# A four-layer transformer on one core: the fourth layer's preparation moved among and behind the third layer's expert blocks, and a tail with two buffers

## The chip, the cores and the metric

The kernel runs on one core of a Trainium2 chip. The metric is device time in microseconds from launch to end; lower is better. Before the change the median of three runs is 1811.25 us (1808.31 to 1811.31).

## The reference, cut to what matters

A token stream `x` of 8 x 256 tokens with 128 features goes through four layers. Each layer adds a cross attention of the normalised tokens and then a feed forward of the normalised result. The change touches the end of the third layer's feed forward (eight experts, two of them for each token) and what the fourth layer needs before its attention can start:

```python
x = x + _L2_ffn_ref(_layernorm(x), gate_w, w1, w3, w2)
#   scores = softmax(x @ gate_w.T); the two best experts, weights p0 and p1
#   each expert: y = (silu(x @ w1.T) * (x @ w3.T)) @ w2.T
#   result per token: p0 * y_first + p1 * y_second
x = x + _L3_xattn_ref(_layernorm(x), ctx_768, mask, g_norm, null_kv, Wq, Wkv, Wout, g_out)
x = x + _L3_ffn_ref(_layernorm(x), W_fc, b_fc, A_fc, B_fc, W_proj, b_proj, A_proj, B_proj)
#   W_fc and W_proj: rounded to 8 bits with one scale each, plus a low rank term
```

## The kernel before, in words

Each engine has a program of its own, and semaphores order them. TensorE (`pe`), ScalarE (`act`), VectorE (`dve`), GpSimd (`pool`) and SyncE (`sp`) run through the same list: `attention(n)`, `feed_forward(n)`, then `early(n + 1)` (the parts of the next layer that don't need its tokens), then on TensorE and ScalarE `ffn_end(n)` (the last normalised tokens), then `boundary`, where all wait for all. An engine executes its instructions in the order in which they are written; a wait holds everything behind it on that engine.

**The blocks.** The third layer's feed forward (`routed_by_token`, L1336 for GpSimd, L1551 ScalarE, L2051 TensorE, L2703 VectorE) works on 39 blocks of 128 token rows, each belonging to one expert. For a block, SyncE loads the rows (`block_rows_at`, L994, L1004), TensorE turns them (L1647, a transposition), ScalarE rounds them to f16 (L1409), VectorE takes the remainder (L2731), TensorE multiplies with two weight matrices (18 matmuls), ScalarE takes the silu (L1568), VectorE the product (L2736), TensorE multiplies with the third matrix (3 matmuls, which the profile records as 6), VectorE copies the result to SBUF (`y_of`, L2758), and GpSimd stores it to its tokens' places in HBM with an indirect DMA (L1342). Rings of eight hold the rows and the results: SyncE loads block i into a place only when the store of block i - 8 has landed, since the store takes its addresses from that place, and VectorE copies result i only when store i - 8 has landed.

**The token tail.** When all stores have landed, SyncE loads the results back, 512 tokens (a chunk) at a time, two transfers each (L1011), with two places in SBUF. For each of the four chunks VectorE forms the sum in `xnew` (L2747, L2751, four instructions each), takes the statistics (L2262, L2267, into `mv`) and copies `xnew` to `x` (L2756); GpSimd turns the variance into a factor (L1072, L1073) and writes the normalised rows to `yn` (L1076, four instructions); TensorE turns them into bank 6 (`turn_rows`, L1922); ScalarE writes them to `xnT` (`ffn_ln_evac`, L879). `xnew`, `mv` and `yn` exist once: VectorE waits for `yn` of a chunk before the next chunk's sum.

**The fourth layer's preparation.** `early(ATT[3])` comes behind the tail on VectorE and GpSimd. On TensorE it starts when three of the four chunks are in `xnT` (a wait in `attention`, L1735, on `f.lne`), because the tail's turns stand ahead of it; `ffn_end` then turns the fourth chunk behind it. In it:
- VectorE takes the largest absolute value of a weight part for each partition (L2368), and GpSimd takes it across partitions (`partition_all_reduce`, L1113); VectorE forms scales from it (`value_scale`, `values_scale_and_ones`, L2376), for which ScalarE and VectorE wait to evacuate the values.
- TensorE fills two key and two value tiles; ScalarE and VectorE evacuate them.
- `prep3_operands` (L2334) on VectorE: two maxima (L2336, L2337), for which GpSimd's second `partition_all_reduce` (L1116) waits, two copies, a product and a sum for the null key (L2343, L2345), two small ones, and the rounding of two weights in three instructions each (L2351 to L2353).
- `prep_fill` (L1675) and `evacuate_prep` (L2392): five fills on TensorE in the order bfc, bpr, nv, fc, pr, each evacuated by ScalarE (bfc, nv, pr) or VectorE (bpr, fc). fc and pr take 8 matmuls each, in the profile 16 records, half of them with 16 rows, and wait for the rounded weights.

Of the kernel before, what the change touches and what calls it, by code (L numbers as in the profile page):

```python
# [311 lines left out]
def build(nc, a, out):  # L312
    ctx = ExitStack()
    with ctx:
# [177 lines left out]
        yg2 = Qf[:, 1568:3616].rearrange("p (c j t d) -> p c j t d", j=2, t=4, d=D)  # L492
        yb2 = PTs[:, :, :].rearrange("p u s -> p (u s)")[:, 0:1024].rearrange("p (r d) -> p r d", d=D)
# [531 lines left out]
        def _(pool):  # L1025
# [82 lines left out]
            def early(A):  # L1108
                if A.n == 0:
                    first_context(A)  # L1110
                if A.n == 3:
                    pool.wait_ge(vmax3_rows, 1)
                    pool.partition_all_reduce(vmaxall[:, 3:4], vmax[:, 3:4], P, RMAX).then_inc(vmax3_max, 1)  # L1113

                    pool.wait_ge(prep3_rows, 1)
                    pool.partition_all_reduce(amx, am, P, RMAX).then_inc(prep3_max, 1)  # L1116
# [219 lines left out]
            def routed_by_token(F):  # L1336
# [3 lines left out]
                for i in range(nb):  # L1340
                    need(pool, r.y_read, i + 1)
# [3 lines left out]
                for c in range(NCH):  # L1345
                    if c:
                        need(pool, s.lnf, c)
                    normalise(4, s.stats, c + 1, s.yn, 1.0 + EPS, EPS * EPS, link)
# [54 lines left out]
        def _(act):  # L1403
# [147 lines left out]
            def routed_by_token(F):  # L1551
# [18 lines left out]
                for c in range(NCH - 1):  # L1570
                    need(act, s.lnf, c + 1)
                    ffn_ln_evac(F, move, c).then_inc(s.lne.sem, 1)
# [50 lines left out]
            def ffn_end(F):  # L1623

                s = ffn_s[F.n]
                need(act, s.lnf, NCH if F.n == 2 else NCH + 1)
                ffn_ln_evac(F, move, NCH - 1).then_inc(s.lne.sem, 1)
# [13 lines left out]
        def _(pe):  # L1641
# [93 lines left out]
            def attention(A, early=None):  # L1735
# [9 lines left out]
                elif A.n:  # L1745

                    f = ffn_s[A.n - 1]
                    need(pe, f.lne, NCH - 1 if A.n == 3 else NCH)
# [173 lines left out]
            def turn_rows(F, c):  # L1922
# [128 lines left out]
            def routed_by_token(F):  # L2051
# [188 lines left out]
        def _(dve):  # L2240
# [93 lines left out]
            def prep3_operands():  # L2334
                dve.wait_ge(prep3_zero, 1)
                dve.tensor_reduce(am[:, 0:1], fcn, AX.X, ALU.max, apply_absolute_value=True)  # L2336
                dve.tensor_reduce(am[:, 1:2], prn, AX.X, ALU.max,  # L2337
                                  apply_absolute_value=True).then_inc(prep3_rows, 1)
                dve.tensor_copy(NVflat[0:64, 0:128:18], nv_col[0:64, 0:1].to_broadcast([64, 8]))
                dve.tensor_copy(NVflat[64:128, 1:128:18],  # L2340
                                nv_col[64:128, 0:1].to_broadcast([64, 8])).then_inc(prep3_done, 1)
                q3 = qtmp.rearrange("p (h e) -> p h e", e=64)
                link(dve.tensor_tensor(q3, L3Wq.rearrange("p (h e) -> p h e", e=64),  # L2343
                                       nk_bc[:, :].unsqueeze(1).to_broadcast([P, 16, 64]), ALU.mult))
                link(dve.tensor_reduce(Wn, q3, AX.X, ALU.add))  # L2345
                dve.wait_ge(prep3_max, 1)
                link(dve.tensor_scalar(qsc, amx, 1.0 / 127.0, None, ALU.mult))
# [566 lines left out]
```

## Time and profile before

| | us |
|---|---|
| median of 3 runs | 1811.25 |
| the profiled execution's own time | 1810.04 |
| its span, first to last instruction | 1808.2 |
| last expert matmul ends | 1304.6 |
| first chunk's sum starts | 1311.5 |
| the last chunk is in `xnT` | 1377.05 |
| fourth layer's queries start | 1377.14 |

Engine names: PE is TensorE's matmuls, PEld its weight loads, DVE VectorE, ACT ScalarE, POOL GpSimd, SPq SyncE's DMA queue. Times are from the span's start. A timeline row gives start, duration, engine, line, operation, output and inputs, the count of merged instructions, and in brackets the engine's idle time before it and what ended it.

### The profile page before, as it was taken

How to read it: one execution, taken by the hardware profiler on the slowest of the kernel's cores; microseconds unless marked ns; L12 is line 12 of the kernel's file. 1: busy time of each engine (PE TensorE's matmuls, PEld its weight loads, DVE VectorE, ACT ScalarE, POOL GpSimd, SP SyncE). 2: the span in 40 equal slices, each digit the busy share in tenths (PEclk: the TensorE clock that was granted, in tenths of full speed). 3: DMA queues.
4: the chain of work that ended last, by engine and by line, in shares of the span. 5: the costliest groups of instructions: out<-in, count | busy, mean ns of one | idle time of the engine just before them, and what ended most of it. 6: DMA issues, size and time to landing. Idle time of an engine off the chain costs nothing. (4 is left out here: it accounts for less than half of the span.)

```text
span 1808.2 us, 38603 instructions
## 1 busy us (share of the span) xinstructions
PE 1438.6 (80%) x12662; PEld 1092.6 (60%) x12662; DVE 1105.0 (61%) x2873; ACT 835.5 (46%) x1870; POOL 417.5 (23%) x743
## 2 busy tenths in 40 slices
PE   4989999978999679999628347378728988888977
PEld 2667777756666468887416235356515766667765
DVE  4757777775666668888421136623244888887761
ACT  1545665554333357777315223122203666656542
POOL 2000000011000323332030245723230122222221
PEclk9999999999999889999759768589957999999989
DMA  8980000000000300000011002111110000000000
GB/s 231 284 25 0 0 0 0 0 1 1 1 0 0 96 1 1 0 0 1 1 35 45 24 12 61 40 44 46 45 34 1 2 1 0 0 0 0 1 1 24
DMA packets 81168, 47.91 MB, mean 26 GB/s; under 512 B 27497, under 2 KB 74226, under 8 KB 80882
## 3 DMA queue, kind: packets, MB, share of 16 engines
q1 hardware_dynamic: 77778, 39.86, 10.2%
q0 software_dynamic: 3296, 6.82, 1.1%
q8 instruction: 56, 0.92, 0.2%
q14 instruction: 38, 0.31, 0.1%
HBM read 26.52 MB, written 20.14 MB: 26 GB/s over the span
## 5 line engine op out<-in xcount | busy, mean ns | idle before, releaser
L1451 ACT ACTIVATE Pm<-bank,negm 128x256 f32<-128x256 f32 x784 | 322.5, 473 | 309.6 <-DVE negm L2454 219.6
L1643 PE MATMUL bank<-kT,Qz 64*128 64x256 f32 (+2 forms) x1568 | 298.2, 404 | 10.9 <-ACT Pm L1451 7.4
L2465 DVE TENSOR_TENSOR PTs<-bank,PTs 128x512 f16<-128x512 f32 x384 | 251.4, 683 | 33.3 <-ACT PTs L1409 32.2
L1647 PE MATMUL bank<-ident,Pm 128*128 128x128 f32 x1568 | 230.8, 283 | 43.8 <-DVE PTs L2465 39.2
L1647 PEld LDWEIGHTS bank<-ident,Pm 128*128 128x128 f32 x1568 | 175.8, 143 | 114.4 <-issue 80.1
L1643 PEld LDWEIGHTS bank<-kT,Qz 64*128 64x128 f32 (+1 forms) x1568 | 183.5, 189 | 84.4 <-issue 49.7
L2454 DVE TENSOR_REDUCE negm<-bank 128x2 f32<-128x512 f32 x264 | 176.5, 687 | 79.8 <-PE bank L1643 77.2
L1409 ACT ACTIVATE PTs<-bank 128x512 f16<-128x512 f32 (+1 forms) x388 | 218.7, 604 | 3.5 <-PE bank L1647 3.4
L1643 PEld LDWEIGHTS bank<-VxF,PTs 128*128 128x128 f16 (+1 forms) x4672 | 183.4, 100 | 11.4 <-DVE PTs L2465 3.4
L1643 PE MATMUL bank<-VxF,PTs 128*128 128x65 f16 (+3 forms) x4672 | 187.9, 189 | 2.5 <-DVE PTs L2465 2.4
L1643 PE MATMUL bank<-Qz,R 128*128 128x128 f16 x978 | 92.5, 231 | 29.0 <-ACT Qz L1409 25.1
L1643 PEld LDWEIGHTS bank<-Qz,R 128*128 x978 | 70.1, 99 | 57.5 <-issue 44.9
L1643 PE MATMUL bank<-xHL,R 128*128 (+1 forms) x432 | 99.2, 379 | 0.9 <-DVE Qz L2846 0.8
L1647 PE MATMUL bank<-ident,yn 128*128 128x128 f32 x120 | 27.9, 347 | 90.2 <-POOL yn L1076 86.2
L2451 DVE TENSOR_REDUCE negm<-bank 128x2 f32<-128x512 f32 x128 | 88.2, 689 | 17.4 <-PE bank L1643 15.5
L1129 POOL TENSOR_TENSOR Qz<-xnT,headmask 128x1024 f32<-128x1024 f32 x32 | 60.5, 1894 | 147.3 <-PE bank L1643 129.3
L1643 PE MATMUL bank<-xnT,R 128*128 (+2 forms) x288 | 88.0, 435 | 8.2 <-DVE VxF L795 6.2
L1076 POOL TENSOR_SCALAR yn<-xnew,mv,rstd 128x128 f32<-128x128 f32 x112 | 90.2, 813 | 9.4 <-POOL rstd L1073 9.4
L1643 PEld LDWEIGHTS bank<-R,Qz 128*128 128x128 f32 x704 | 84.1, 192 | 11.1 <-ACT Qz L1611 6.4
L1072 POOL TENSOR_SCALAR ve<-mv 128x2 f32<-128x2 f32 (+1 forms) x44 | 8.9, 203 | 354.3 <-DVE mv L2267 327.7
L1643 PE MATMUL bank<-R,Qz 128*128 128x128 f32 x704 | 85.1, 276 | 3.1 <-ACT Qz L1611 3.1
L1604 ACT ACTIVATE Pm<-bank,upback 128x512 f32<-128x512 f32 x72 | 49.6, 689 | 78.0 <-PE bank L1643 77.8
(327 smaller groups left out, 2168.1 us busy)
## 6 DMA issues: line engine op xcount, KB each, us to landing
token_rows_by_expert<-trash SPq DMA_DIRECT2D x5, 1782.0 KB, 17.9
Qz<-token_rows_by_expert SPq DMA_DIRECT2D x39, 66.0 KB
token_rows_by_expert<-wpad SPq DMA_DIRECT2D x10, 256.0 KB, 4.2
R<-in_L_ffn_ew SPq DMA_DIRECT2D x2, 1024.0 KB, 7.2
R<-in_L_ffn_w SPq DMA_DIRECT2D x1, 2048.0 KB, 9.6
Qz<-expert_rows_by_token SPq DMA_DIRECT2D x8, 256.0 KB, 3.3
R<-in_L_xattn_Wkv SPq DMA_DIRECT2D x2, 768.0 KB, 6.6
Qz<-token_rows_by_expert SPq DMA_DIRECT2D x23, 64.0 KB
```

The source lines that it names most:

```text
L1072: chain(pool.tensor_scalar(ve[:, 0:n], mv[:, at:at + n, 1], scale, offset, ALU.mult, ALU.add))
L1076: last = pool.tensor_scalar(yn[:, at + t, :], xnew[:, at + t, :], mv[:, at + t, 0:1], rstd[:, t:t + 1], ALU.subtract, ALU.mult)
L1129: pool.tensor_tensor(Qz[:, h:h + 4, :], xnT[:, bass.ts(bw, S)].unsqueeze(1).to_broadcast([P, 4, S]), headmask[:, h:h + 4].unsqueeze(2).to_ ...
L1409: return act.activation(dst, src, ACT.Copy, scale=1.0 if gain is None else gain)
L1451: last = act.activation(Pm[:, k % 4, qt * S:(qt + 1) * S], bank[k % 2][:, qt * S:(qt + 1) * S], ACT.Exp, bias=negm[:, k % 4, qt:qt + 1])
L1604: act.activation(sg[0:M, u % 2, :], bank[u % 2][0:M, :], ACT.Silu, scale=upback[0:M, F.n:F.n + 1]).then_inc(s.silu.sem, 1)
L1643: return pe.matmul(o, l, r, start=start, stop=stop)
L1647: return pe.transpose(o, i, ident[0:n, 0:n])
L2451: chain(dve.tensor_reduce(nm, v, AX.X, ALU.max, negate=True))
L2454: dve.tensor_reduce(nm, v, AX.X, ALU.max, negate=True).then_inc(s.negmax.sem, 1)
L2465: dve.tensor_tensor(PTl[:, k % 4, :], bank[2 + k % 2][:, :], PTh[:, k % 4, :], ALU.subtract).then_inc(s.pt[1].sem, 1)
```

## The change

VectorE's `early` parts for the fourth layer become `prep3_part(i)`, called once at the end of each block's iteration on VectorE; most numbers of i do nothing. GpSimd's two `partition_all_reduce` stand ahead of its store of block 10. TensorE's and ScalarE's handling of all four chunks of the tail moves behind `early(ATT[3])`, VectorE's `token_tail` too; GpSimd's part stays where it was. In numbers: `prep3_part` 3 is L2368, 4 and 5 the maxima L2336 and L2337, 6 the two small copies, 7 and 8 L2343 and L2345, 20 and 21 the scales, 22 to 27 the rounding (the old `prep3_operands` is cut up for it and left out below). Sums, statistics and normalised rows have two buffers, so that VectorE and GpSimd each wait for the chunk before the last one.

```diff
@@ -490,6 +490,10 @@
+        mv8 = sb("mv8", [P, 2, 4, 2])
+        spare = PTs[:, :, :].rearrange("p u s -> p (u s)")
+        xn8 = (xnew, spare[:, 1024:1536].rearrange("p (t d) -> p t d", d=D))
+        yn8 = (yn, spare[:, 1536:2048].rearrange("p (t d) -> p t d", d=D))
@@ -1108,12 +1112,6 @@
             def early(A):
                 if A.n == 0:
                     first_context(A)
-                if A.n == 3:
-                    pool.wait_ge(vmax3_rows, 1)
-                    pool.partition_all_reduce(vmaxall[:, 3:4], vmax[:, 3:4], P, RMAX).then_inc(vmax3_max, 1)
-
-                    pool.wait_ge(prep3_rows, 1)
-                    pool.partition_all_reduce(amx, am, P, RMAX).then_inc(prep3_max, 1)
@@ -1338,14 +1336,26 @@
                 for i in range(nb):
+                    if i == 10:
+                        pool.wait_ge(vmax3_rows, 1)
+                        pool.partition_all_reduce(vmaxall[:, 3:4], vmax[:, 3:4], P, RMAX).then_inc(vmax3_max, 1)
+                        pool.wait_ge(prep3_rows, 1)
+                        pool.partition_all_reduce(amx, am, P, RMAX).then_inc(prep3_max, 1)
                     need(pool, r.y_read, i + 1)
                     pool.indirect_dma_start(out=ytok, out_offset=bass.IndirectOffsetOnAxis(
                         ap=xb2[:, i % RING, D:D + 1].bitcast(U32), axis=0),
...
                 for c in range(NCH):
-                    if c:
-                        need(pool, s.lnf, c)
-                    normalise(4, s.stats, c + 1, s.yn, 1.0 + EPS, EPS * EPS, link)
+                    need(pool, s.stats, c + 1)
+                    plain(pool)
+                    link(pool.tensor_scalar(ve[:, 0:4], mv8[:, c % 2, :, 1], 1.0 + EPS, EPS * EPS, ALU.mult, ALU.add))
+                    link(pool.tensor_tensor(rstd[:, 0:4], ve[:, 0:4], neghalf[:, 0:4], ALU.pow))
+                    need(pool, s.lnf, c - 1)
+                    plain(pool)
+                    for t in range(4):
+                        last = pool.tensor_scalar(yn8[c % 2][:, t, :], xn8[c % 2][:, t, :], mv8[:, c % 2, t, 0:1],
+                                                  rstd[:, t:t + 1], ALU.subtract, ALU.mult)
+                    last.then_inc(s.yn.sem, 1)
@@ -1567,9 +1577,6 @@
-                for c in range(NCH - 1):
-                    need(act, s.lnf, c + 1)
-                    ffn_ln_evac(F, move, c).then_inc(s.lne.sem, 1)
@@ -1623,6 +1630,10 @@
                 s = ffn_s[F.n]
+                if F.n == 2:
+                    for c in range(NCH - 1):
+                        need(act, s.lnf, c + 1)
+                        ffn_ln_evac(F, move, c).then_inc(s.lne.sem, 1)
                 need(act, s.lnf, NCH if F.n == 2 else NCH + 1)
                 ffn_ln_evac(F, move, NCH - 1).then_inc(s.lne.sem, 1)
@@ -1745,7 +1756,7 @@
-                    need(pe, f.lne, NCH - 1 if A.n == 3 else NCH)
+                    need(pe, f.lne, 0 if A.n == 3 else NCH)
                     if A.n - 1 in ROUTED:
@@ -1924,7 +1935,7 @@
-                    last = turn(bank[6][:, t * P:(t + 1) * P], yn[:, t, :])
+                    last = turn(bank[6][:, t * P:(t + 1) * P], (yn8[c % 2] if F.n == 2 else yn)[:, t, :])
                 last.then_inc(s.lnf.sem, 1)
@@ -1933,6 +1944,11 @@
+                if F.n == 2:
+                    for c in range(NCH - 1):
+                        need(pe, ffn_s[F.n].lne, c)
+                        turn_rows(F, c)
+                    need(pe, ffn_s[F.n].lne, NCH - 1)
                 turn_rows(F, NCH - 1)
@@ -2099,14 +2115,6 @@
-                for c in range(NCH - 1):
-                    if c:
-                        need(pe, s.lne, c)
-                    else:
-                        need(pe, r.high, nb)
-                        need(pe, r.low, nb)
-                    turn_rows(F, c)
@@ -2331,26 +2339,42 @@
-            def prep3_operands():
...
+            def prep3_part(i):
+                if i == 3:
+                    loaded(dve, "l3")
+                    dve.wait_ge(prep3_zero, 1)
+                    dve.tensor_reduce(vmax[0:DC, 3:4], L3Wkv[:, 1024:2048], AX.X, ALU.max,
+                                      apply_absolute_value=True).then_inc(vmax3_rows, 1)
+                elif i == 4:
+                    dve.tensor_reduce(am[:, 0:1], fcn, AX.X, ALU.max, apply_absolute_value=True)
+                elif i == 5:
+                    dve.tensor_reduce(am[:, 1:2], prn, AX.X, ALU.max,
+                                      apply_absolute_value=True).then_inc(prep3_rows, 1)
+                elif i == 6:
...
+                elif i == 7:
+                    link(dve.tensor_tensor(q3, L3Wq.rearrange("p (h e) -> p h e", e=64),
...
+                elif i == 8:
+                    link(dve.tensor_reduce(Wn, q3, AX.X, ALU.add))
+                elif i == 20:
+                    dve.wait_ge(prep3_max, 1)
+                    link(dve.tensor_scalar(qsc, amx, 1.0 / 127.0, None, ALU.mult))
+                    link(dve.reciprocal(rqs, qsc))
+                elif i == 21:
+                    values_scale_and_ones(ATT[3])
+                elif 22 <= i < 28:
+                    n, w = (i - 22) // 3, (fcn, prn)[(i - 22) // 3]
+                    if (i - 22) % 3 == 0:
+                        link(dve.tensor_scalar(w, w, rqs[:, n:n + 1], ROUND, ALU.mult, ALU.add))
+                    elif (i - 22) % 3 == 1:
+                        link(dve.tensor_scalar(w, w, -ROUND, 127.0, ALU.add, ALU.min))
+                    else:
...
@@ -2363,13 +2387,7 @@
             def early(A):
-                if A.n == 3:
-                    loaded(dve, "l3")
-                    dve.tensor_reduce(vmax[0:DC, 3:4], L3Wkv[:, 1024:2048], AX.X, ALU.max,
-                                      apply_absolute_value=True).then_inc(vmax3_rows, 1)
                 attention(A, ("early",))
-                if A.n == 3:
-                    prep3_operands()
                 if A.n in prep:
                     evacuate_prep(A)
@@ -2423,7 +2441,7 @@
-                        if kinds == "early" and (kind, k) == ("v", 0):
+                        if kinds == "early" and (kind, k) == ("v", 0) and A.n != 3:
                             values_scale_and_ones(A)
@@ -2738,22 +2756,33 @@
                     if i >= 2:
                         y_of(r, i - 2)
+                    prep3_part(i)
                 y_of(r, nb - 1)
+            def token_tail(F):
...
                 for c in range(NCH):
-                    need(dve, s.yn, c)
+                    xn = xn8[c % 2]
+                    need(dve, s.yn, c - 1)
                     dve.wait_ge(r.tail[c % 2], 16 * 2 * (c // 2 + 1))
                     for t in range(4):
-                        last = dve.scalar_tensor_tensor(xnew[:, t, :], yg2[:, c % 2, 0, t, :], c_p0[:, 4 * c + t:4 * c + t + 1],
+                        last = dve.scalar_tensor_tensor(xn[:, t, :], yg2[:, c % 2, 0, t, :], c_p0[:, 4 * c + t:4 * c + t + 1],
...
                         last.then_inc(r.added.sem, 1)
                     need(dve, r.added, 4 * c + 4)
-                    stats(xnew, 4, link, s.stats.sem)
-                    link(dve.tensor_copy(x[:, 4 * c:4 * c + 4, :], xnew[:, :, :]))
+                    plain(dve)
+                    for t in range(4):
+                        last = dve.bn_stats(st6[:, t, :], xn[:, t, :])
+                    link(last)
+                    for t in range(4):
+                        last = dve.bn_aggr(mv8[:, c % 2, t, :], st6[:, t, :])
+                    last.then_inc(s.stats.sem, 1)
+                    dve.tensor_copy(x[:, 4 * c:4 * c + 4, :], xn[:, :, :])
@@ -2893,6 +2922,8 @@
                     early(ATT[n + 1])
+                    if n == 2:
+                        token_tail(FFN[n])
                     boundary(dve, "dve", n + 2)
```

## Rows read from the trace of the kernel before

**Rows 1.** The timeline, last block: its last expert matmuls.
```profile
1303.68 0.93 PE L1643 MATMUL bank<-R,Pm 128*128 x6 [0.48 <-DVE Pm L2736]
```
**Rows 2.** The timeline, token tail: chunk one, starts of chunks two and four.
```profile
1307.66 15.82 SPq L1011 DMA_DIRECT2D Qz<-expert_rows_by_token  x8
1311.52 1.14 DVE L2747 SCALAR_TENSOR_TENSOR xnew<-Qz,OT,x 128x128 f32<-128x128 f32 x4 [6.58 <-DMA Qz<-expert_rows_by_token]
...
1315.47 0.19 POOL L1072 TENSOR_SCALAR ve<-mv 128x4 f32<-128x4 f32 x1 [9.24 <-DVE mv L2267]
...
1317.01 3.13 POOL L1076 TENSOR_SCALAR yn<-xnew,mv,rstd 128x128 f32<-128x128 f32 x4 [0.22 <-POOL rstd L1073]
1320.23 1.14 DVE L2747 SCALAR_TENSOR_TENSOR xnew<-Qz,OT,x 128x128 f32<-128x128 f32 x4 [4.66 <-issue]
...
1337.93 1.14 DVE L2747 SCALAR_TENSOR_TENSOR xnew<-Qz,OT,x 128x128 f32<-128x128 f32 x4 [4.62 <-issue]
```
**Rows 3.** The timeline, preparation of the fourth layer: fills, first reduce, evacuation of fc.
```profile
1339.90 3.75 PE L1643 MATMUL bank<-ctxT,R 97*128 97x256 f32 x8 [0.83 <-issue]
...
1343.89 3.78 PE L1643 MATMUL bank<-R,ctxb 96*128 96x512 f32 x4 [0.24 <-DVE kT L2252]
...
1352.23 0.38 POOL L1113 PARTITION_ALL_REDUCE vmaxall<-vmax  x1 [5.71 <-issue]
...
1356.34 1.23 PE L1647 MATMUL bank<-ident,R 128*16 128x128 f32 x5 [8.66 <-DVE VxF L795]
...
1358.02 3.51 PE L1643 MATMUL bank<-R 128*16 128x128 f32 x16 [0.46 <-ACT R L1409]
...
1368.77 0.69 DVE L2252 COPY R<-bank 128x512 f32<-128x512 f32 x1 [5.15 <-PE bank L1643]
```
**Rows 4.** The timeline, last chunk's turn and evacuation, first queries.
```profile
1375.21 1.12 PE L1647 MATMUL bank<-ident,yn 128*128 128x128 f32 x4 [0.69 <-ACT R L1409]
1376.36 0.69 ACT L1410 ACTIVATE xnT<-bank,vecT 128x512 f32<-128x512 f32 x1 [1.21 <-PE bank L1647]
1377.14 5.14 PE L1643 MATMUL bank<-xnT,R 128*128 128x256 f32 x12 [0.81 <-ACTq L665]
```
**Rows 5.** The timeline at full clock: a key fill, a value fill.
```profile
1384.23 1.13 PE L1643 MATMUL bank<-ctxT,R 97*128 97x256 f32 x4
...
1389.78 1.02 PE L1643 MATMUL bank<-R,ctxb 96*128 96x512 f32 x2
```
**Rows 6.** Windows: length, busy of PE PEld DVE ACT POOL, PEclk, DMA share, GB/s.
```profile
1304.60:1306.60 2.00, 0.01 (x1) 0.00 (x0) 0.29 (x1) 0.00 (x0) 1.33 (x2) 1.00 0.10 33
1365.00:1374.50 9.50, 9.50 (x27) 6.49 (x26) 0.69 (x1) 0.00 (x0) 0.00 (x0) 0.50 0.00 0
1374.50:1381.50 7.00, 5.50 (x15) 4.25 (x15) 0.00 (x0) 2.43 (x4) 0.40 (x1) 0.50 0.01 2
```
**Rows 7.** The timeline, the third layer's attention: VectorE and GpSimd at the same time.
```profile
1109.79 0.45 DVE L2502 TENSOR_TENSOR xnew<-rtmp,x 128x256 f32<-128x256 f32 x1
1109.79 1.82 POOL L1076 TENSOR_SCALAR yn<-xnew,mv,rstd 128x128 f32<-128x128 f32 x2 [0.22 <-POOL rstd L1073]
```
**Rows 8.** Within the blocks, timeline: product, turn, store, load; tile view: all stores.
```profile
1212.91 0.62 DVE L2736 SCALAR_TENSOR_TENSOR Pm<-bank,upback,Pm 128x384 f32<-128x384 f32 x1 [2.11 <-ACT Pm L1568]
...
1213.04 0.27 PE L1647 MATMUL bank<-ident,Qz 128*128 128x128 f32 x1
...
1214.00 0.96 POOL L1342 DMA_INDIRECT expert_rows_by_token<-PTs,Qz  x1 [2.22 <-DVE PTs L2762]
...
1216.47 0.34 SPq L1004 DMA_DIRECT2D Qz<-token_rows_by_expert  x1
...
L1342 POOL DMA_INDIRECT expert_rows_by_token<-PTs,Qz x39: 959/960/988, 1189.4 to 1305.3; - x39
```
**Rows 9.** VectorE's longest part in the timeline, and a window over most parts.
```profile
1357.66 1.23 DVE L2343 TENSOR_TENSOR R<-R,nk_bc 128x1024 f32<-128x1024 f32 x1
...
1356.11:1363.44 7.33, 4.74 (x21) 2.75 (x21) 7.01 (x16) 0.85 (x2) 0.39 (x1) 0.64 0.00 0
```

More of the change, by code:

```diff
@@ L2332, in _ @@
             boundary(dve, "dve", 1)
-            def prep3_operands():
[L2335 to L2341, printed above, removed]
-                q3 = qtmp.rearrange("p (h e) -> p h e", e=64)
[L2343 to L2347, printed above, removed]
-                link(dve.reciprocal(rqs, qsc))
-                for i, w in enumerate((fcn, prn)):
-                    link(dve.tensor_scalar(w, w, rqs[:, i:i + 1], ROUND, ALU.mult, ALU.add))
-                    link(dve.tensor_scalar(w, w, -ROUND, 127.0, ALU.add, ALU.min))
-                    dve.tensor_scalar(w, w, -128.0, qsc[:, i:i + 1], ALU.max, ALU.mult).then_inc(prep3_done, 1)
@@ new lines, in prep3_part @@
+            def prep3_part(i):
+                q3 = qtmp.rearrange("p (h e) -> p h e", e=64)
+                if i == 3:
[9 more added lines that the diff above has]
+                elif i == 6:
+                    dve.tensor_copy(NVflat[0:64, 0:128:18], nv_col[0:64, 0:1].to_broadcast([64, 8]))
+                    dve.tensor_copy(NVflat[64:128, 1:128:18],
+                                    nv_col[64:128, 0:1].to_broadcast([64, 8])).then_inc(prep3_done, 1)
+                elif i == 7:
+                    link(dve.tensor_tensor(q3, L3Wq.rearrange("p (h e) -> p h e", e=64),
+                                           nk_bc[:, :].unsqueeze(1).to_broadcast([P, 16, 64]), ALU.mult))
+                elif i == 8:
[13 more added lines that the diff above has]
+                    else:
+                        dve.tensor_scalar(w, w, -128.0, qsc[:, n:n + 1], ALU.max, ALU.mult).then_inc(prep3_done, 1)
@@ L2740, in routed_by_token @@
                         y_of(r, i - 2)
+                    prep3_part(i)
                 y_of(r, nb - 1)
+            def token_tail(F):
+                s, r = ffn_s[F.n], routed_s[F.n]
                 for c in range(NCH):
-                    need(dve, s.yn, c)
+                    xn = xn8[c % 2]
+                    need(dve, s.yn, c - 1)
                     dve.wait_ge(r.tail[c % 2], 16 * 2 * (c // 2 + 1))
                     for t in range(4):
-                        last = dve.scalar_tensor_tensor(xnew[:, t, :], yg2[:, c % 2, 0, t, :], c_p0[:, 4 * c + t:4 * c + t + 1],
+                        last = dve.scalar_tensor_tensor(xn[:, t, :], yg2[:, c % 2, 0, t, :], c_p0[:, 4 * c + t:4 * c + t + 1],
                                                         x[:, 4 * c + t, :], ALU.mult, ALU.add)
@@ L2750, in routed_by_token @@
                     for t in range(4):
-                        last = dve.scalar_tensor_tensor(xnew[:, t, :], yg2[:, c % 2, 1, t, :], c_p1[:, 4 * c + t:4 * c + t + 1],
-                                                        xnew[:, t, :], ALU.mult, ALU.add)
+                        last = dve.scalar_tensor_tensor(xn[:, t, :], yg2[:, c % 2, 1, t, :], c_p1[:, 4 * c + t:4 * c + t + 1],
+                                                        xn[:, t, :], ALU.mult, ALU.add)
                         last.then_inc(r.added.sem, 1)
                     need(dve, r.added, 4 * c + 4)
-                    stats(xnew, 4, link, s.stats.sem)
-                    link(dve.tensor_copy(x[:, 4 * c:4 * c + 4, :], xnew[:, :, :]))
+                    plain(dve)
[6 more added lines that the diff above has]
+                    dve.tensor_copy(x[:, 4 * c:4 * c + 4, :], xn[:, :, :])
             def y_of(r, j):
```

## Prediction

> **What bounds the kernel now.** I read the page first: no engine is full, so a stage has to be read by its own waits. Then the timeline from the last expert matmul to the first query. The last expert matmuls end at 1304.6 [rows 1], and the fourth layer's queries start at 1377.14 [rows 4]: 72.5 us, and nothing of the fourth layer's attention can start before their end. Two chains stand one behind the other in it. The first is the token tail [rows 2]: the stored rows come back at 1311.5, and from one chunk's sum to the next are (1337.93 - 1311.52) / 3 = 8.8 us, in which VectorE works 3.95 us (1311.52 to 1315.47), GpSimd 4.67 us (1315.47 to 1320.14), and each waits for the other, since `xnew` and `yn` exist once. The second is the preparation [rows 3]: it begins at 1339.9 on TensorE, and until 1375.2 [rows 4] it is a chain through all engines, with 5.71 us before the `partition_all_reduce` in which GpSimd shows no instruction. TensorE's clock is at 0.50 in nearly all of it [rows 6], that is at 1.2 GHz of 2.4. The blocks before it are another matter: there TensorE sets a period of (1305.3 - 1189.4) / 38 = 3.05 us, and VectorE waits 2.11 us at a stretch in each [rows 8].
>
> **The change, part by part.** The sum is made from 1304.6, the end of the blocks, to the queries' start, and compared with 72.5 us.
>
> VectorE's parts among the blocks. A part stands behind the copy of a result and ahead of the remainder L2731 of the next block. That remainder is next used by the following period's matmuls, nearly a period later, and the product L2736 comes after an idle stretch of 2.11 us [rows 8]. The longest part takes 1.23 us [rows 9], so each fits; I cost them at nothing. Without that cover they would cost 7.33 us for the window over most parts [rows 9], 1.2 for L2368 (as large as L2343), 1.15 for the scales, together 9.7 us.
>
> GpSimd's hold at block 10. The two reductions stand ahead of store 10. Their price is 5.71 + 0.38 [rows 3], then about 0.8 for the second and gaps: 7 us, if the second doesn't pay 5.7 again. Store 9 would end near 1218, store 10 start near 1225 instead of 1220. What waits: SyncE's load of block 18 and VectorE's copy 18. Store 8 starts at 1214.0 and the load of block 16 at 1216.5 [rows 8]; VectorE is then two blocks behind TensorE's turns, so the turn of block 11 is the one at 1213.04, and that of block 16 comes five periods later, at 1228.3. A load lands within 3 us, so the slack is about 9 us; a hold that delays store 10 by 5 us is hidden. With a second 5.7 us it would be 10.7, a loss of 1 to 2 us. Nothing taken; the removed 5.71 + 0.38 at the old place are in the 72.5.
>
> The preparation, now directly behind the blocks. TensorE's fills start at about 1304.8. Unmoved at the old speed they are: keys 3.75, values 3.8, evacuation of the last value 1.8 (two instructions of 0.9 on ScalarE, then VectorE), bfc and bpr to nv's start 1.7 (1356.34 to 1358.02), nv 3.5, fc 16 records at 9.50 / 27 = 0.35 us, so 5.6, and VectorE's evacuation 0.7 [rows 3, 6]: 20.9 us, so that VectorE is free at 1325.7. At full clock a key fill is 1.13 and a value fill 1.02 [rows 5], so 2.3 and 2.0, nv half, fc 3.4 (half and a start): 13.8 us, free at 1318.6. Which clock? It stays at 1.00 for two us after the last matmul [rows 6], and now TensorE goes on working; but in the same preparation fc and pr ran at 0.50 although TensorE was busy all 9.50 us [rows 6]. So I take the fills at full clock and fc at half, the row nearest to it, free at 1320.7. pr follows on TensorE and is hidden by the tail. The rows from HBM (1311.5) are there before that: their latency costs nothing now.
>
> The tail with two buffers. VectorE's 4.2 us for a chunk (with the copy) is now beside GpSimd's 4.67, and GpSimd's is longer. With 0.1 for a wait: 3.95 + 4 x 4.75 = 22.95, then 0.15, the turn 1.12, the evacuation 0.69 and 0.1 to the queries [rows 4]: 25.0 us. The loads of chunks three and four wait for `added` of the chunk two before (2.3 us into it) and take 4 us: hidden.
>
> VectorE and GpSimd now work at once, as they never did in the tail. In the third layer's attention they do [rows 7]: two L1076 beside a VectorE instruction with two inputs in SBUF took 1.82 us, where two in the tail take 1.57 [rows 2], so 0.25 us more for 0.45 us of VectorE. VectorE's sums are 2.3 us a chunk, with the copy 2.7. If GpSimd lost all of it for three chunks it would be 8 us, at the least nothing. By that ratio [rows 7] it would be up to 1.5 a chunk, but only part of the sums falls beside L1076; I take 0.7 a chunk, 2.1 us.
>
> The clock after it. TensorE is now idle in most of the tail. Before, it rose only at 1381.5, 4.4 us after the queries' start, although fc and pr had gone before [rows 6]. It can come later now. Between 0 and 3 us (the queries' 5.14 us [rows 4] at half clock, and some more), I take 1.
>
> The sum: 1304.6 + 16.1 (preparation) + 25.0 + 2.1 = 1347.8, against 1377.1: 29.3 us less, less 1 for the clock: 28.3. Against the profiled execution's own time, 1810.04, that gives 1781.7; the median, 1811.25, is 1.2 above it, and gives 1783. I predict 1782.5. Own bounds: full clock, no contention, no loss, 33.5 less, 1777; half clock throughout, contention and 3 us of clock, 1304.8 + 20.9 + 25.0 + 8 = 1358.7, so 15.4 less, 1796; not all of these fall together, so about 1776 to 1790.
>
> **The rivals.**
>
> *The tail doesn't overlap.* VectorE's two input sums and GpSimd's normalisation exclude each other, so that a chunk still costs near 8.8 us. For it: the longer L1076 [rows 7]. Against it: there only a part of VectorE's time was lost. The tail is then 3 x 8.8 + 8.6 + 2.1 = 37.1 instead of 27.1: 10 us less gained, 1792.5. The Trainium skill (SBUF — State Buffer, "Who interferes with whom") says that a VectorE instruction with two SBUF inputs contends with a GpSimd instruction that reads SBUF, through a shared read interface held for the whole instruction. By that rule as a strict lock, all of the sums and the copy would come on top of GpSimd's time, 8 us for three chunks where I take 2.1, and the sum would be 1788.5; the trace shows a part of it [rows 7].
>
> *The blocks grow.* The parts aren't free among the blocks, 9.7 us, or the hold is longer than its cover. For it: the store's engine holds for 7 us, and VectorE's parts stand ahead of L2731, which TensorE waits for. Against it: idle 2.11 us in each period. 1782.5 + 9.7 = 1792.
>
> *Slower than before: the clock stays down.* TensorE idles from about 1326 to 1348 but for turns, and the fourth layer's first batch, which begins behind it, runs at 1.2 GHz. To eat 28 us, matmuls that are busy 28 us at full clock would have to take double: a stretch at half clock of some 60 us behind the queries' start instead of 4.4. In the rows the longest such stretch is 1365.0 to 1381.5, 16.5 us [rows 6]. At 70 us it would give about 1815.
>
> *The change doesn't do what it says.* A wait left ahead of the preparation would keep it behind the tail. `need` with the value 0 gives no wait, the loads of the fourth layer's weights stand ahead of the blocks' loads in SyncE's program, and the memsets that part 3 waits for stand ahead of the stores in GpSimd's. Only the two buffers would be left, three times 8.8 - 4.75, 12 us less: 1799. Very small.
>
> **How the numbers follow.** The forecast 0.68; the tail without overlap 0.14; the blocks grow 0.10; the preparation kept behind 0.02; the clock 0.03; unnamed small mixtures of the first three 0.03. The range must take in the first rival's neighbourhood in part: 1774 to 1792 leaves out the far ends of both rivals and what is above, about 0.2. A measurement of this kernel can tell about 0.2%, 3.6 us, from no change; only the clock case ends above that, and of what I can't name 0.01 within it: faster 0.96, same 0.01, slower 0.03.
>
> **What would show it.** In the changed profile: the block period still 3.05 us and the last expert matmul near 1304.6; a gap in GpSimd's stores behind store 9 of about 8 us with the next four close together, and no later turn waiting for a load; the key fills directly behind the last block with the clock at 1.00; the first sum near 1321 with nothing waited for but fc's evacuation; sums and normalisation side by side with a period near 5.5 us, set by GpSimd; queries near 1348. It would be wrong if the first sum stands behind 1326, if L1076's successor takes well over 0.8 us each, if the period is near 8, or if the clock rises more than 8 us behind the queries' start.

## The result, and where the time went

The changed kernel takes 1789.88 us (median of 4 runs, 1787.96 to 1791.18), the kernel before 1811.2 beside it: ratio 0.988, 95% interval 0.9867 to 0.9893. The time lies within the range, but of the 28.7 us that the prediction took off, 21.3 came. So the question is where 7.4 us went.

I read the timeline over the same stretch as before, from the last expert matmul to the first query. TensorE's part of the preparation, now directly behind the blocks:

```profile
1307.48 0.93 PE L1654 MATMUL bank<-R,Pm 128*128 x6 [0.48 <-DVE Pm L2754]
1308.25 1.89 PE L1654 MATMUL bank<-ctxT,R 97*128 97x256 f32 x8
...
1315.14 3.56 PE L1654 MATMUL bank<-R 128*16 128x128 f32 x16 [0.56 <-ACT R L1419]
...
1321.55 0.48 PE L1654 MATMUL bank<-R 16*128 16x128 f32 x2
...
1321.96 0.80 PE L1654 MATMUL bank<-ident,R 128*128 128x128 f32 x2
1322.07 0.69 DVE L2260 COPY R<-bank 128x512 f32<-128x512 f32 x1 [7.17 <-PE bank L1654]
1322.68 1.13 DVE L2770 SCALAR_TENSOR_TENSOR xnew<-Qz,OT,x 128x128 f32<-128x128 f32 x4
```

The last expert matmuls end at 1308.41. The key fills stand right behind them and take 1.89 us instead of 3.75 [rows 3]: full clock. The windows (the number behind the five engines is the granted clock) show that it isn't kept throughout:

```profile
1308.40:1315.10 6.70, 4.35 (x18) 2.24 (x16) 2.89 (x7) 2.76 (x6) 1.32 (x2) 1.00 0.41 117
1315.10:1318.50 3.40, 3.36 (x16) 2.24 (x16) 0.00 (x0) 0.00 (x0) 0.00 (x0) 0.50 0.42 117
1318.50:1322.00 3.50, 3.50 (x19) 2.40 (x17) 0.00 (x0) 0.27 (x1) 0.00 (x0) 0.99 0.00 0
```

nv runs at half clock and takes 3.56 us, as before (3.51 [rows 3]). fc falls into the stretch at full clock behind it, where a pair of matmuls takes 0.48 to 0.49 us; from 1321.96 on, in pr, a pair takes 0.80 again. The first sum stands directly behind VectorE's evacuation of fc (a line with no wait in brackets), 14.3 us behind the last expert matmul. Then the tail, GpSimd and the two ends of the chain:

```profile
1326.04 0.38 DVE L2783 BATCH_NORM_AGGREGATE mv<-st 128x2 f32<-128x6 f32 x4
...
1333.67 0.19 POOL L1351 TENSOR_SCALAR ve<-mv 128x4 f32<-128x4 f32 x1 [23.65 <-issue]
...
1335.22 3.16 POOL L1356 TENSOR_SCALAR yn<-xnew,mv,rstd 128x128 f32<-128x128 f32 x4 [0.22 <-POOL rstd L1352]
1338.41 1.14 DVE L2770 SCALAR_TENSOR_TENSOR xnew<-Qz,OT,x 128x128 f32<-128x128 f32 x4 [7.72 <-POOL yn L1356]
...
1343.53 1.14 DVE L2770 SCALAR_TENSOR_TENSOR PTs<-Qz,OT,x 128x128 f32<-128x128 f32 x4 [0.95 <-POOL PTs L1356]
...
1345.28 3.74 POOL L1356 TENSOR_SCALAR yn<-xnew,mv,rstd 128x128 f32<-128x128 f32 x4 [0.24 <-POOL rstd L1352]
...
1350.65 3.12 POOL L1356 TENSOR_SCALAR PTs<-PTs,mv,rstd 128x128 f32<-128x128 f32 x4 [0.24 <-POOL rstd L1352]
...
1355.04 0.69 ACT L1420 ACTIVATE xnT<-bank,vecT 128x512 f32<-128x512 f32 x1 [4.06 <-PE bank L1658]
1359.86 4.33 PE L1654 MATMUL bank<-xnT,R 128*128 128x256 f32 x12 [4.86 <-POOLq L669]
```

Here are both losses. First, the statistics of chunk one are there at 1326.42, but the first factor L1351 starts at 1333.67, and "issue" says that nothing in the profile is waited for: 7.0 us beyond a usual 0.2. Second, the last xnT ends at 1355.73, but the queries start at 1359.86 and wait for POOLq L669; before, they waited for ACTq L665, 0.09 us behind it [rows 4]. The view by line of these two lines names them:

```profile
L1351 POOLq MODIFY_POOL_CONFIG  x2: 11/11/11, 1326.7 to 1326.7; - x2
...
L669 POOLq DRAIN  x1: 8934/8934/8934, 1350.7 to 1350.7; - x1
```

I take the idle time behind MODIFY_POOL_CONFIG for the loading of the code of another group of GpSimd operations; experiments 1, 3 and 5 test it. The record alone isn't the price: at 163.05 one stands 0.13 us ahead of the tensor_scalar at 163.18. The reductions among the blocks had loaded their code; the stores behind them need none, and the first tensor_scalar after them loads its own back. It starts to do so at 1326.65, because the wait for the statistics stands ahead of it in GpSimd's program. The kernel before shows the same way back in its second layer, with a reduction at 916.05 and nothing but indirect DMAs between it and this row:

```profile
1034.71 0.19 POOL L1072 TENSOR_SCALAR ve<-mv 128x4 f32<-128x4 f32 x1 [7.13 <-issue]
```

Without a reduction ahead of them the 39 stores cost nothing of the kind: the first factor of the kernel before waits for its statistics alone [rows 2].

At the layer's boundary, the second loss, every engine waits for the drains of all; GpSimd's ends near 1359.7, 5.9 us behind its last instruction (1353.77). Before, a drain of 6.3 us stood there too, from 1357.4, beside the chain of the preparation, where nobody waited for it.

GpSimd among the blocks, the hold at block 10:

```profile
1220.90 0.96 POOL L1345 DMA_INDIRECT expert_rows_by_token<-PTs,Qz  x1 [2.13 <-DVE PTs L2791]
1228.32 0.38 POOL L1341 PARTITION_ALL_REDUCE vmaxall<-vmax  x1 [6.46 <-issue]
1228.61 0.44 POOL L1343 PARTITION_ALL_REDUCE R<-R  x1
1229.24 1.20 POOL L1345 DMA_INDIRECT expert_rows_by_token<-PTs,Qz  x1 [0.19 <-issue]
...
1233.38 0.96 POOL L1345 DMA_INDIRECT expert_rows_by_token<-PTs,Qz  x1 [0.41 <-DVE PTs L2791]
```

From store 9 to store 10 are 8.3 us; with store 13 it has caught up, and no turn waited. The period is (1309.06 - 1193.36) / 38 = 3.04 us, as before, with the clock at 1.00 in all of it: VectorE's parts are hidden.

In one sum, over the two profiled executions: from the last expert matmul's end to the queries 72.5 us became 51.45, 21.1 less; from there to the end of the span 431.1 became 429.6, 1.4 less; ahead of the last expert matmul the new execution is 3.8 us later, and 3.7 of it are there already at the first load of a block. The stages ahead of that load were not changed, and over all kernels here but experiment 5 the end of the last expert matmul scatters between 1302.8 and 1308.4 us. So I compare stretches from the last expert matmul on, beside the times.

### The profile page after: what moved, and what is told of

It is laid out like the page before. It is cut to its first block, busy times and chain, and to the rows that moved or that the text cites. A ratio compares the mean times of both kernels' runs of the same rounds, so it can differ in the third digit from the quotient of the medians.

```text
span 1789.5 us, 38608 instructions
## 1 busy us (share of the span) xinstructions
PE 1435.3 (80%) x12662; PEld 1092.5 (61%) x12662; DVE 1104.2 (62%) x2873; ACT 833.5 (47%) x1870; POOL 418.3 (23%) x743
## 3 DMA queue, kind: packets, MB, share of 16 engines
q1 hardware_dynamic: 77778, 39.86, 10.2%
## 4 chain that ended last, share of the span: by engine, by line
PE 58%; DVE 16%; issue 11%; POOL 6%; ACT 5%; SPq 1%; POOLq 1%; DMA 1%; DVEq 0%; ACTq 0%
PE bank L1654 48%; PE bank L1658 10%; DVE PTs L2483 3%; DVE negm L2469 2%; DVE negm L2472 2%; DVE VxF L799 1%; ACT Pm L1461 1%; SPq L893 1%; POOL token_rows_by_expert L1141 1%; DVE st L2270 1%; ACT PTs L1419 1%; ACT Pm L1552 1%; POOL token_rows_by_expert L1312 1%; ACT Qz L1419 1%; POOL yn L1080 1%
## 5 line engine op out<-in xcount | busy, mean ns | idle before, releaser
L1654 PEld LDWEIGHTS bank<-R,Qz 128*128 128x128 f32 x704 | 84.1, 192 | 11.1 <-ACT Qz L1618 6.4
L1419 ACT ACTIVATE Qz<-bank 128x128 f16<-128x128 f32 (+1 forms) x102 | 41.7, 409 | 95.9 <-PE bank L1658 72.9
```

The lines of the kernel that those rows point to most:

```text
L1419: return act.activation(dst, src, ACT.Copy, scale=1.0 if gain is None else gain)
L1654: return pe.matmul(o, l, r, start=start, stop=stop)
```

## The experiments

All start from the changed kernel. "Stretch" is the time from the last expert matmul's end to the queries' start, in the profiled execution: 51.45 us in the changed kernel. Beside experiments 1 to 4 the kernel before took 1809.03 us (median of 7), beside experiments 5 to 8 1810.41 (of 9); each ratio is to the kernel before beside it.

**1. Load the code back early.** One small tensor_scalar on GpSimd behind the last store; its result is overwritten before it is read.

```diff
                         in_=yb2[:, i % RING, :], in_offset=None).then_inc(r.stored[i % RING].sem, 16)
+                link(pool.tensor_scalar(ve[:, 0:4], neghalf[:, 0:4], 1.0, 0.0, ALU.mult, ALU.add))
                 for c in range(NCH):
```

> The changed kernel with one small tensor_scalar added on GpSimd behind its last store, where it then idles for over 20 us. Theory (code swap): in the changed kernel the first factor of the tail starts 7.0 us after the statistics it waits for, and a MODIFY_POOL_CONFIG stands in that gap, because the two reductions among the blocks left other code on GpSimd. The small instruction takes this gap into the idle stretch: the first factor follows its statistics within 0.3 us, the tail is 7 us shorter, about 1783 us. Rival (the indirect DMAs are still being finished, or GpSimd is slow to wake after a long wait): the gap stays, the same 1790 us.

GpSimd in its timeline:

```profile
1311.70 0.19 POOL L1348 TENSOR_SCALAR ve<-neghalf 128x4 f32<-128x4 f32 x1 [6.93 <-issue]
1320.95 0.20 POOL L1352 TENSOR_SCALAR ve<-mv 128x4 f32<-128x4 f32 x1 [9.05 <-DVE mv L2784]
```

The 6.93 us of "issue" now stand beside TensorE's fills, and the first factor starts 0.2 us behind its statistics. Stretch 45.2 us, 6.2 less. Time 1782.68 us (1780.9 to 1789.07, 4 runs), ratio 0.9863 (0.9837 to 0.989). The queries still wait 4.86 us for POOLq L669.

**2. Drain early.**

```diff
                         in_=yb2[:, i % RING, :], in_offset=None).then_inc(r.stored[i % RING].sem, 16)
+                pool.drain()
                 for c in range(NCH):
```

> The changed kernel with one more drain on GpSimd behind its last store, ahead of the tail. Theory (drain pays for indirect DMAs): GpSimd's drain at the boundary ends 5.9 us after its last instruction, with 71 indirect DMAs since the drain before; at the third layer's boundary 2.7 us with 32; at the second none with none: about 0.083 us each. With a drain in the idle stretch the one at the boundary ends with the last instruction, and the queries start 4.1 us earlier, right behind the last evacuation: about 1786 us. Rival (a drain on GpSimd costs about 6 us there by itself): nothing changes at the boundary, 1790 us.

The boundary's drain and the queries:

```profile
L669 POOLq DRAIN  x1: 3121/3121/3121, 1349.7 to 1349.7; - x1
```

```profile
1332.63 0.19 POOL L1352 TENSOR_SCALAR ve<-mv 128x4 f32<-128x4 f32 x1 [23.54 <-issue]
...
1354.75 2.50 PE L1655 MATMUL bank<-xnT,R 128*128 128x256 f32 x5 [0.81 <-ACTq L669]
```

The boundary's drain is now as long as the last yn beside it, and the queries wait for ScalarE again. The load of the code is still there. Stretch 47.3 us, 4.2 less. Time 1785.93 us (1780.52 to 1788.59, 4 runs), ratio 0.986 (0.9834 to 0.9886); by the times alone it could not be told from experiment 1.

**3. Both**, the drain first, then the small instruction.

> Both additions together, drain and then the small tensor_scalar. If both theories hold the gains add: 7.0 + 4.1 = 11.1 us, about 1779 us, and from the last expert matmul to the queries there are 40.3 us instead of 51.4. By the rivals between 1783 and 1790.

```profile
1317.24 0.19 POOL L1349 TENSOR_SCALAR ve<-neghalf 128x4 f32<-128x4 f32 x1 [12.78 <-issue]
1320.65 0.20 POOL L1353 TENSOR_SCALAR ve<-mv 128x4 f32<-128x4 f32 x1 [3.21 <-DVE mv L2785]
...
1322.21 3.91 POOL L1358 TENSOR_SCALAR yn<-xnew,mv,rstd 128x128 f32<-128x128 f32 x4 [0.22 <-POOL rstd L1354]
...
1327.89 3.77 POOL L1358 TENSOR_SCALAR PTs<-PTs,mv,rstd 128x128 f32<-128x128 f32 x4 [0.21 <-POOL rstd L1354]
...
1333.45 3.74 POOL L1358 TENSOR_SCALAR yn<-xnew,mv,rstd 128x128 f32<-128x128 f32 x4 [0.24 <-POOL rstd L1354]
...
1338.83 3.13 POOL L1358 TENSOR_SCALAR PTs<-PTs,mv,rstd 128x128 f32<-128x128 f32 x4 [0.24 <-POOL rstd L1354]
```

12.78 us of "issue", the drain's 5.9 and the code's 6.9, lie in GpSimd's idle time, and 3.21 us of it are left ahead of the first factor. Stretch 41.2 us: 10.3 less, where the two alone gave 6.2 + 4.2 = 10.4. They add up, so each was a cost of its own. Time 1779.98 us (1776.97 to 1782.3, 4 runs), ratio 0.9841 (0.9822 to 0.986).

**4. How long is the drain for what?** The drain ahead of store 0 instead, so that of the layer's 71 indirect DMAs the 32 that spread the token rows over the experts are drained early and the 39 stores are not.

```diff
                 for i in range(nb):
+                    if i == 0:
+                        pool.drain()
```

> The changed kernel with one more drain on GpSimd ahead of its store of block 0, none behind the stores. 39 indirect DMAs then lie between it and the boundary's drain. Theory (0.083 us each): the boundary's drain ends 3.2 us after the last normalised row instead of 5.9, and the queries start 2.6 us earlier against the last evacuation. Rival (a drain before takes the whole cost away, or none of it): 0 or 5.9 us.

```profile
L669 POOLq DRAIN  x1: 6313/6313/6313, 1346.7 to 1346.7; - x1
```

It ends at 1353.0, the last yn at 1349.8: 3.3 us behind it. With the 71 of the changed kernel it is 5.9, with the 32 at the third layer's boundary 2.7, with the 32 ahead of the new drain here 2.7 again, with none 0.1. So about 0.083 us for each indirect DMA issued since the drain before. All of them move 128 rows, so these runs can't tell a count of DMAs from a count of rows. Stretch 49.0 us, 2.4 less, where 2.6 was expected. One run, 1786.51 us.

**5. A longer hold.** Experiment 3, and the small tensor_scalar between the two reductions, so that the code is changed three times at block 10.

```diff
                         pool.partition_all_reduce(vmaxall[:, 3:4], vmax[:, 3:4], P, RMAX).then_inc(vmax3_max, 1)
+                        link(pool.tensor_scalar(ve[:, 0:4], neghalf[:, 0:4], 1.0, 0.0, ALU.mult, ALU.add))
                         pool.wait_ge(prep3_rows, 1)
```

> The kernel with both additions, and one more small tensor_scalar between the two reductions at block 10, so that GpSimd swaps its code three times there: about 20 us of hold instead of 8. It tests the slack that I gave the loads. Theory (a load may come 9 us late): store 10 is 18 us late instead of 5, and the blocks lose 18 - 9 = 9 us, in one gap before the turn of block 18. Rival (the ring of eight covers it, or the store is on the chain at once): no loss, or 13 us more than now.

```profile
1225.43 0.38 POOL L1341 PARTITION_ALL_REDUCE vmaxall<-vmax  x1 [5.98 <-issue]
...
1233.57 0.19 POOL L1343 TENSOR_SCALAR ve<-neghalf 128x4 f32<-128x4 f32 x1 [7.77 <-issue]
...
1239.55 0.37 POOL L1344 PARTITION_ALL_REDUCE R<-R  x1 [5.79 <-issue]
1240.12 1.20 POOL L1346 DMA_INDIRECT expert_rows_by_token<-PTs,Qz  x1 [0.19 <-issue]
...
1244.63 0.45 PE L1661 MATMUL bank<-ident,Qz 128*128 128x128 f32 x1 [8.37 <-DMA Qz<-token_rows_by_expert]
1245.53 2.10 PE L1657 MATMUL bank<-Qz,R 128*128 128x128 f16 x18 [0.45 <-ACT Qz L1422]
```

Each change of code costs 5.8 to 7.8 us, in either direction, and no indirect DMA stands between them. Store 10 starts at 1240.1 instead of near 1221.6 without any hold (store 9 at 1218.5 and one period), so 18.5 us late, and the turn of block 18 waits 8.37 us for its load, where 9 was worked out. From the first store to the last are 124.2 us instead of 115.8 in experiment 3. So the chain store, load, turn is as the prediction took it, and the slack is about 10 us where it had 9. Behind the gap the 18 matmuls take 2.10 us instead of 1.6: the granted clock is 0.50 from 1241.0 to 1251.2. One run, 1784.68 us against 1779.98 for experiment 3: the blocks' 8.4 us don't show in full, since in that execution the stretch is 1.6 us shorter (39.6) and the part behind it 2.4 (428.8 instead of 431.2).

**6. Take the first chunk ahead.** Experiment 3 has GpSimd idle until the first statistics, which wait for fc's evacuation. Here VectorE takes the first chunk between the evacuations of bpr and of fc, and the small instruction stands ahead of store 20, where the stores have slack.

```diff
+                    if i == 20:
+                        link(pool.tensor_scalar(ve[:, 0:4], neghalf[:, 0:4], 1.0, 0.0, ALU.mult, ALU.add))
...
-                if A.n in prep:
+                if A.n == 3:
+                    evacuate_prep(A, 2)
+                    token_tail(FFN[2], (0,))
+                    evacuate_prep(A, 5, 2)
+                elif A.n in prep:
                     evacuate_prep(A)
```

> The kernel with both additions, and two more edits: VectorE does the first chunk's sum and statistics between its evacuations of bpr and fc, where it idles for 7 us, and GpSimd's small tensor_scalar stands ahead of store 20, so that the code swap lies among the blocks. Theory (the tail is a chain of GpSimd's four normalisations, 20 us, behind the first statistics): the first sum starts when its rows have come back, about 6.9 us behind the last expert matmul instead of 13.9, and the whole tail is 7 us earlier: 33 us from the last expert matmul to the queries, about 1773 us. Rival (the preparation on TensorE, or the turns behind it, sets the end): the first turn waits for the fills, and no more than 2 us are won, 1778 us or more.

```profile
1309.82 1.12 DVE L2777 SCALAR_TENSOR_TENSOR xnew<-Qz,OT,x 128x128 f32<-128x128 f32 x4
...
1313.74 0.19 POOL L1354 TENSOR_SCALAR ve<-mv 128x4 f32<-128x4 f32 x1 [9.25 <-DVE mv L2790]
...
1316.12 0.69 DVE L2263 COPY R<-bank 128x512 f32<-128x512 f32 x1 [2.27 <-PE bank L1657]
1316.73 1.17 DVE L2777 SCALAR_TENSOR_TENSOR PTs<-Qz,OT,x 128x128 f32<-128x128 f32 x4
...
1320.82 0.19 POOL L1354 TENSOR_SCALAR ve<-mv 128x4 f32<-128x4 f32 x1 [2.20 <-DVE mv L2790]
```

Stretch 35.7 us, 5.5 less than experiment 3 where 8 was expected: the second chunk's sum now waits for fc (1316.12), so GpSimd idles 2.2 us behind the first. Of the expectation's two cases, the tail's chain set most of the gain and the preparation the rest. No turn waits behind the small instruction at store 20. Time 1772.49 us (1770.83 to 1774.18, 5 runs), ratio 0.979 (0.9776 to 0.9804): faster than both kernels, and the best of this study.

**7. No overlap.** Experiment 3 with the sum of a chunk behind the normalisation of the one before, the buffers still two.

```diff
-                    need(dve, s.yn, c - 1)
+                    need(dve, s.yn, c)
```

> The kernel with both additions, but VectorE waits for the normalised rows of the chunk before, as with single buffers. It prices the two buffers. Theory (two buffers hide VectorE's 4 us under GpSimd's 5): the period goes from 5.4 back to 8.7 us, three times 3.3, 10 us slower than with both additions, about 1790 us, and L1358's four instructions take 3.13 us each time instead of 3.7 to 3.9, since nothing runs beside them. Rival (VectorE and GpSimd exclude each other): 3 us slower or less.

```profile
1325.75 3.16 POOL L1358 TENSOR_SCALAR yn<-xnew,mv,rstd 128x128 f32<-128x128 f32 x4 [0.22 <-POOL rstd L1354]
1328.95 1.14 DVE L2772 SCALAR_TENSOR_TENSOR PTs<-Qz,OT,x 128x128 f32<-128x128 f32 x4 [4.62 <-POOL yn L1358]
...
1337.56 1.14 DVE L2772 SCALAR_TENSOR_TENSOR xnew<-Qz,OT,x 128x128 f32<-128x128 f32 x4 [4.56 <-POOL PTs L1358]
```

The period is 8.6 us (8.8 in the kernel before), VectorE waits 4.6 us for GpSimd and GpSimd 4.0 for VectorE, and the stretch is 50.8 us, 9.6 more than in experiment 3. Time 1786.27 us (1784.2 to 1787.9, 4 runs), ratio 0.986 (0.9842 to 0.9878): 6.3 us more than experiment 3 by the medians, 3.4 by the ratios, whose intervals overlap, so the 9.6 rest on the profiles. It is also the measure of the contention: alone, a chunk's four instructions take 3.12 to 3.16 us.

**8. VectorE's parts without spreading.** Experiment 3 with parts 3 to 8 all at block 8.

```diff
-                    prep3_part(i)
+                    if i == 8:
+                        for part_ in range(3, 9):
+                            prep3_part(part_)
+                    elif i > 8:
+                        prep3_part(i)
```

> The kernel with both additions, but VectorE's six parts 3 to 8 all at block 8, 5.5 us at once instead of 1.3 at most. Theory (cover of one period: the remainder is needed 2.8 us after it ends, and VectorE's idle stretch is 2.1 us): TensorE waits once, by 5.5 - 2.8 = 2.7 us, and the blocks grow by that. Rival (the parts are paid whatever their place): no change, since they were paid before; or all 5.5 us show.

```profile
1212.00 1.22 DVE L2365 TENSOR_REDUCE R<-R 128x16 f32<-128x1024 f32 x1
1213.25 0.29 DVE L2751 TENSOR_TENSOR Qz<-bank,Qz 128x128 f16<-128x128 f32 x1
...
1213.74 2.10 PE L1656 MATMUL bank<-Qz,R 128*128 128x128 f16 x18 [2.96 <-DVE Qz L2751]
```

TensorE waits 2.96 us for the remainder that stands behind the parts, and the granted clock is 0.50 from 1212.9 to 1219.7, about two blocks. From store to store are 6.1, 3.3 and 3.3 us (starts 1208.41, 1214.54, 1217.84, 1221.11) instead of 3 x 3.1, about 3.4 us lost; from the first store to the last it is 118.6 us instead of 115.8 in experiment 3, 2.8 more, where 2.7 was expected. The one run's time, 1779.95 us, doesn't show it: the start of the stage scatters by as much. It is the cover that makes the parts free: one at a time fits in VectorE's idle stretch, six don't.

## Why the prediction was right, and what it missed

**The mechanism held.** The parts among the blocks cost nothing (period unchanged, and experiment 8 shows the price without spreading). The hold at block 10 was hidden (8.3 us from store to store, forecast about 8), with the slack near what was worked out (experiment 5: about 10 us, 9 worked out). The preparation came directly behind the blocks, and the tail overlaps (experiment 7: 9.6 us are its worth, where the first rival put 10).

**The step that failed: GpSimd's change of code was costed once.** The prediction priced the 5.7 us ahead of the reductions at block 10 and asked what the stores behind them wait for, but not what GpSimd must do to get from the reductions back to tensor_scalar. In the kernel before, the reductions stood behind the last yn, and that way back lay outside the path. There a copy ran without it (1377.21, 0.4 us), the load began at 1377.64 and the next tensor_tensor, at 1386.08, waited for VectorE anyway. Moved ahead of the tail, it falls into the first chunk: 7.0 us. Experiment 1 takes it away and gets 6.2 back. The price could have been read ahead of the change, from the second layer's 7.13 us. The Trainium skill (GPSIMD Engine Reference, "2.1 Instruction dispatch") says that the first call of freshly loaded code pays a load of some 6 us without a visible instruction; the traces agree, with 5.7 to 7.8 us at eight such places (6.46 and 7.0 in the changed kernel, 6.93, 5.98, 7.77 and 5.79 in experiments 1 and 5, and 5.71 [rows 3] and 7.13 before), and show that it is paid each way.

**The second: the boundary's drain was taken as hidden, which it had been.** It took 6.3 us in the kernel before, and ended 13 us ahead of the queries. The prediction asked of each stall what is late next, but for the stretch between the last yn and the queries it only took ScalarE's rows [rows 4]. It cost 4.1 us; experiment 2 gets 4.2 back.

**Sizes.** The preparation up to the first sum took 14.3 us instead of 16.1. The forecast had the fills and nv at full clock and fc at half; it came the other way round for the last two: nv took 3.56 us at half clock where half of 3.5 was put in, and fc and its evacuation's start 3.4 where 5.6 was. The row that fc's price was taken from [rows 6] begins at 1365.0, but fc began at 1363.67, and its first two pairs took 0.49 and 0.48 us there too: in the kernel before the clock was at 1.00 from 1361.3 to 1364.7, and for 2.14 us of that fc still waited for VectorE. Now fc stands right behind nv and uses that stretch (1318.5 to 1322.0).

From the first factor to the last yn's end are 20.1 instead of 21.1 us. The stall of the code had let VectorE finish the second chunk, so less fell side by side; in experiment 3, without it, it is 21.3. There the contention is (3.91 + 3.77 + 3.74) - 3 x 3.13 = 2.0 us, and 2 x 0.16 for the factors L1353, 2.3 in all where 2.1 was forecast. The Trainium skill (SBUF — State Buffer, "Who interferes with whom") calls the shared port an exclusive lock. The 8 us of the prediction's lock don't test that, because only part of VectorE's 2.7 us a chunk falls beside L1358: in experiment 3 that is 0.80, 0.58 and 0.56 us of the sums and 0.4 of each copy, 3.1 in all, of which 2.0 come on top. Experiment 6 does test it: there 2.4 us of sums, a whole chunk's, run beside the first L1359.

```profile
1315.30 3.33 POOL L1359 TENSOR_SCALAR yn<-xnew,mv,rstd 128x128 f32<-128x128 f32 x4 [0.22 <-POOL rstd L1355]
1317.93 1.26 DVE L2781 SCALAR_TENSOR_TENSOR PTs<-Qz,OT,PTs 128x128 f32<-128x128 f32 x4
```

GpSimd takes 3.33 us instead of 3.13, and VectorE 1.17 and 1.26 us instead of 1.12 and 1.14. Where the page has a lock, these rows show two engines at work side by side, each a little slower; what decides how much each loses is not shown.

The clock behind the tail was put at 1 us more, and from the queries to the end it is 1.4 us less. No effect of the change can be read from that: in the changed kernel and the eight experiments, whose code is the same there, this part takes 428.8 to 432.0 us (431.1 before), the queries' twelve matmuls 4.25 to 5.49 us (5.14 before), and the granted clock comes back to 1.00 between 2.8 and 6.1 us behind their start (4.6 before, 3.1 after). The rival that the clock stays down fell: it is at 1.00 from 1362.9 on.

**The sum.** The forecast was 28.3 us less in the profile. The two waits take 7.0 and 4.1 us of that away; the preparation gives back 1.8, the tail 1.0 and the clock 2.4. So 28.3 - 11.1 + 5.2 = 22.4, and measured are 21.1 + 1.4 = 22.5. That leaves 5.8 us missing behind the last expert matmul; the medians miss 7.4, and the rest is scatter ahead of that point. Of the two rivals nearest to 1789.9, neither was at work: the time lies near theirs (1792) by two waits that no case named. That is why the place of a wait has to be read and not only the time.

**Luck.** The two waits come to 11.1 us, and from the forecast to the end of the range, 1792, are only 9.5. By themselves they would have given about 1793.6. The time is inside because three terms went the other way, and the largest of them, the clock's 2.4 us, is scatter. The chain, the places and the overlap were right; that the number stayed in its range is in part luck. Without the two waits (experiment 3) the kernel takes 1779.98 us, 2.5 below the forecast, or 1782.4 by its ratio 0.9841 to 1811.2.

**What stays open:** why the granted clock falls at 1322.0, and fell at 1364.7 in the kernel before, while TensorE works without a gap; and what the moved preparation and the two buffers are worth apart from each other in the order given here: experiment 7 prices the buffers on top of the moved preparation (9.6 us), and no run has the buffers alone.

## What to carry to other kernels

When an operation is moved on GpSimd, look at what it runs before and after at the new place: a change of the code group cost 6 to 8 us here and as much again on the way back, and a small instruction of the next group in idle time hid it. When a tail becomes shorter, list everything that ran beside it, the boundary's drains too: what was hidden by the old chain may be the new end. When an operation's price is taken from a trace, look for every place where that trace has it, in other layers too. An overlap's worth is best measured by forbidding it in the new kernel, one condition changed.

## What the runs showed of the hardware

- **GpSimd's code groups.** partition_all_reduce on one side and tensor_scalar and tensor_tensor on the other change the code, 5.7 to 6.5 us towards the reductions and 6.9 to 7.8 back at the eight places above. A second reduction right behind the first pays nothing (0.44 us). Indirect stores don't change it: the way back was paid only at the next tensor_scalar, 98 us later. Nor does a copy (0.40 us, behind a reduction, at 1377.21 in the kernel before).
- **A drain on GpSimd counts its indirect DMAs**, though they have long landed: 0.1, 2.7, 3.3 and 5.9 us beyond the last instruction for 0, 32, 39 and 71 of them (of 128 rows each) since the drain before. An early drain in idle time pays for them once (experiment 2: 0.1 us at the boundary instead of 5.9).
- **A short gap costs the clock.** TensorE waited 2.96 us in the blocks (experiment 8), or 8.37 (experiment 5). The granted clock fell from 1.00 to 0.50 within the gap and was back 6.8 and 10.2 us later. The next block had its matmuls at 2.10 and 1.59 us instead of 1.63 and 0.93, the 18 of the one behind it took 2.13: 1.2 GHz instead of 2.4.
- **VectorE and GpSimd side by side.** Four L1358 take 3.12 to 3.16 us alone and 3.74 to 3.91 with the end of VectorE's sums and its copy beside them (experiment 3), but only 3.33 with 2.4 us of sums beside them (experiment 6).
